# Column 1 of the adjacency matrix in two graph layers: taken ahead of time for rows 8 to 15, in each row's own turn for rows 2 to 7

## The chip, the cores and the metric

The kernel runs on one core of a Trainium2 chip. The metric is the time of one execution on the device in microseconds (us); lower is better. The engines are called by the profile's names: PE (TensorE), its weight loads PEld, DVE (VectorE), ACT (ScalarE), POOL (GpSimd) and SP (SyncE, which issues the transfers here).

## What is computed

```python
def reference(x, adj, u, weight, bias):          # x, u: 8192 x 64, adj: 8192 x 8192, fp32
    keep = (u >= 0.1).astype(x.dtype)
    x_drop = x * keep / (1.0 - 0.1)
    h = layernorm(x + jnp.matmul(adj, x_drop))   # over the 64 features, eps 1e-5
    support = jnp.matmul(h, weight)              # weight: 64 x 64
    return layernorm(h + jnp.matmul(adj, support) + bias)
```

The same matrix `adj` (256 MB) is multiplied with two operands of 64 columns, and the second needs the result of the first. The kernel multiplies `adj` with h first and with the weight at the end.

## The kernel before

**Tiles.** `adj` is cut into 16 x 16 tiles (i, j) of 512 x 512 numbers, 1 MB each. SBUF holds 17 of them (`SLOTS`). For a tile the two layers need x_drop of block j (`stat[..., 0:D]`) and h of block j (`stat[..., D:2 * D]`). h of block i exists only after all 16 tiles of row i have been multiplied with x_drop and the row has had its "turn": PE transposes the sum (line 1017), and DVE and ACT add x and normalise (function `turn`, ending in line 751).

**Jobs.** `order_of_work` writes out one list of jobs that all engines follow:

- `first i j`: layer 1's product of a tile (line 949). `second i j` and `pair i j`: layer 2's product of one tile, or of the tiles (i,j) and (i+1,j) (lines 1002, 996), into one of three banks `echo`, from which DVE joins it to `layer2` (line 656).
- `raw i j` and `fused i j`: both products of a tile with j < i from one load. They are made of seven half products instead of eight by the scheme of Strassen and Winograd: `raw` multiplies the tile as it came (lines 931 to 940), DVE makes sums of the tile's quarters (line 680 ahead of it, lines 692 to 697 after it), and `fused` multiplies those (lines 958 to 966). I call the two together a set. A set also needs sums of the operands x and h of block j, which DVE makes once for a block in three steps (`sum_stat`, lines 668 to 672), behind the turn. After a row's last set DVE combines the products (`combine`).
- `early i j`: both products of the tiles (i,j) and (i+1,j), without sums, before row i's own turn to be worked on (line 982), joined to `layer1` and `layer2`. For column 0 most of this is done in still smaller pieces (`chunk`, `rest`).
- `turn i`, `row_end i`, `combine i`, `final i`.

An fp32 matmul instruction stands in the trace as two records, so a `first` is 8 records, a `pair` 16, an `early` 32.

**What sets the order.** Row by row, `order_of_work` puts six halves of filler around the turn of row i-1 (`FILL`), then the seconds with h of block i-1, then mixes what is left: `heavy` (the sets of row i), `light` (its firsts), `again` (seconds of tiles loaded anew) and `early`. Which comes next depends on `lead`, a running account of work against loads (a tile of load counts 16, an `early` 44, a `fused` 19, a `first` 11): when it is low, heavy and early jobs come first. `with_raw` then moves each raw part ahead of the tile job before its fused part. `place_tiles` gives each tile a slot and makes the list of 346 loads that SP issues in the order of first use (line 495); each waits until the job that used the slot before is done.

**Column 1.** `EARLY = 2`: for rows from 2 on, columns 0 and 1 are not part of the row's own work (`begins_at`). Column 1 is taken by seven `early` jobs, `early 2 1`, `early 4 1`, ... `early 14 1`, which go into the list `early` when h of row 1 is due. So a row's sets begin with column 2, and `has_fused(i)` is true from row 3. The operand sums of even blocks have six places in `stat_homes`, those of odd ones lie in parts of `layer1` whose rows are done with.

Of the kernel before, what the change touches and what calls it, by code (L numbers as in the profile page):

```python
# [35 lines left out]
NB = N // B  # L36
# [4 lines left out]

SLOTS = 17
EARLY = 2
HOMES = (NB - 2 - EARLY) // 2
AHEAD = 3
HOLD = 3
FILL = 6
# [62 lines left out]

def begins_at(i):

    return EARLY if i >= EARLY else 0


def has_fused(i):
    return i > EARLY


def double(i, j):  # L120
# [18 lines left out]
def order_of_work():  # L139

    jobs, again, early = [], [], []
    lead = 0

    def put(job):
        nonlocal lead
        if job[0] == "rest":
            n = 0
        elif job[0] in ("first", "both", "fused", "early", "chunk"):  # L150
            n = len(tiles_of(job))
        else:
            n = sum(not held(*tile) for tile in tiles_of(job))
        lead = max(0, min(LEAD_MOST, lead + WORK[job[0]] - n * WORK_OF_LOAD))
        jobs.append(job)

    groups = NB // PARTS
    chunks_due = []
    for q in range(PARTS):
        for g in range(groups):  # L160
            if g == 0 and q in TURN_FIRST:
                jobs.append(("part_turn", q - 1))
            jobs.append(("part", q, g))
            if g == 0 and q and q not in TURN_FIRST:
                jobs.append(("part_turn", q - 1))
            elif g and chunks_due and (q > 1 or g > 1):
                jobs += chunks_due[:2]
                chunks_due = chunks_due[2:]
            if g == 0 and q:
                chunks_due += chunk_jobs(q - 1)  # L170
        jobs.append(("part_end", q))

    pieces = [[job] for job in chunks_due[:len(chunks_due) % 2]]
    pieces += [chunks_due[n:n + 2] for n in range(len(pieces), len(chunks_due), 2)]
    for i in range(1, NB):
        light = [("first", i, j) for j in range(i + 1, NB) if not held(i, j)]
        near = [("first", i, j) for j in range(NB - 1, i - 1, -1) if held(i, j)]
        if i == 1:
            light.insert(0, ("first", 1, 0))
        heavy = [double(i, j) for j in range(begins_at(i), i - 1) if i >= 2]  # L180
        filler, taken, turned = [], 0, False
        while sum(HALVES[job[0]] for job in filler) < FILL:
            choice = [early] if lead < LEAD and early else [again] if i > 7 else []
            choice = [jobs_of for jobs_of in (*choice, light, again, early, heavy, near) if jobs_of]
            if pieces and (i > 1 or len(filler) % 2 == 0):
                filler += pieces.pop(0)
            else:
                filler.append(choice[0].pop(0))
            for job in filler[taken:]:
                put(job)  # L190
            taken = len(filler)
            if not turned:
                turned = True
                jobs.append(("turn", i - 1) if i > 1 else ("part_turn", PARTS - 1))
        if i == 1:
            late = chunk_jobs(PARTS - 1)
            pieces += [[("early", r, 0)] for r in range(rows_of_chunk((NB - EARLY) // PARTS - 1).stop, NB, 2)]
            pieces += [late[n:n + 2] for n in range(0, len(late), 2)]
            used = len(pieces) - KEPT_PIECES
            for n in range(used):  # L200
                for job in pieces.pop(0):
                    put(job)
                for _ in range(len(light) // (used - n)):
                    put(light.pop(0))
        for job in seconds_of([r for r in range(NB) if held(r, i - 1)], i - 1):
            put(job)
        again += seconds_of([r for r in range(i - 1) if not held(r, i - 1)], i - 1)
        if 1 <= i - 1 < EARLY:
            early = sorted(early + [("early", r, i - 1) for r in range(EARLY, NB, 2)], key=lambda job: job[1:])
        if i >= 2 and begins_at(i) < i:  # L210
            heavy.append(double(i, i - 1))
        summed = not has_fused(i)
        kept = LAST_KEPT if i == NB - 1 else AGAIN_KEPT
        in_a_row = 0
        while True:
            due = [job for job in early if job[1] == i]
            if not (heavy or light or due):
                break
            spare = len(light) + max(0, len(again) - kept) + len(early)
            if heavy and in_a_row * (spare + 1) < len(heavy) and in_a_row < MOST_IN_A_ROW:  # L220
                chosen = heavy
            elif lead < LEAD and (due or heavy or early):
                chosen = early if due else (early or heavy if in_a_row >= MOST_IN_A_ROW else heavy or early)
                if chosen is heavy and in_a_row >= MOST_IN_A_ROW:
                    chosen = light or (again if len(again) > kept else heavy)
            elif len(again) > kept:
                chosen = again
            elif i == NB - 1:
                chosen = light or heavy or early
            else:  # L230
                chosen = light or (early if due else heavy)
            in_a_row = in_a_row + 1 if chosen is heavy else 0
            put(chosen.pop(0))
            if not summed and not any(job[0] == "fused" for job in heavy):
                jobs.append(("combine", i))
                summed = True
        for job in near:
            put(job)
        jobs.append(("row_end", i))
    jobs += again[:1]  # L240
    jobs.append(("turn", NB - 1))
    jobs += again[1:]
    pending = None
    for i in range(NB - 2, -1, -2):
        jobs.append(("pair", i, NB - 1))
        if pending is not None:
            jobs.append(("final", pending))
        pending = i
    jobs.append(("final", pending))
    return with_raw(jobs)  # L250
# [46 lines left out]
def resnorm_graph_layers(nc: bass.Bass, x, xu, adj_t, adj_parts, adj_0, adj_chunks, weight, bias, out):  # L297
# [43 lines left out]
    with ctx:  # L341
# [33 lines left out]
        def layer1_pair(i):  # L375
            return layer1[:, (i - EARLY) // 2]

        def stat_sums(j):


            home = layer1_pair(j) if j % 2 else stat_homes[:, (j - EARLY) // 2]
            return home.rearrange("p (v k f) -> p v k f", v=4, k=2)

        def of_part(q):
# [192 lines left out]
        def _(dve):  # L577
# [176 lines left out]
            for job in jobs:  # L754
# [41 lines left out]
                elif job[0] == "row_end":  # L796
                    i = job[1]
                    dve.wait_ge(turned_ready, turns(i - 1))
                    dve.wait_ge(tile_jobs_done, done_after[job])
                    if i < EARLY:  # L800
                        dve.tensor_copy(halves[D:P, :], sum_f[i % 2][D:P, :]).then_inc(half_by_dve, 1)
                    else:

                        dve.wait_ge(added, n_second)
                        dve.tensor_tensor(out=halves[of_row(i), :], in0=sum_f[i % 2][of_row(i), :],
                                          in1=layer1_pair(i)[of_row(i), :], op=ALU.add).then_inc(half_by_dve, 1)
                elif job[0] == "turn":
                    turn(turns(job[1]) - 1, job[1], slice(0, C))
                    if EARLY <= job[1] < NB - 2:
                        sum_stat(job[1])  # L810
                elif job[0] == "final":
                    n = n_final
                    dve.wait_ge(hb_ready, n + 1)
                    dve.wait_ge(product_ready, n + 1)
                    dve.tensor_tensor(out=output_rows(n), in0=product[n % 2][:, :, 0:D], in1=h_bias[n % 2],
                                      op=ALU.add).then_inc(product_read, 1)
                    if n < len(finals) - 2:
                        norms += 1
                        variance(output_squares(n), var[:, n % 2], 2 * C, scale[:, 1:2])
                        if n >= 2:  # L820
                            dve.wait_ge(y_ready, n - 1)
                        inverse_root(rstd[:, n % 2], var[:, n % 2], root[:, n % 2], newton[:, 0], norms).then_inc(rstd_ready, 1)
                    n_final += 1
# [15 lines left out]
        def _(pe):  # L839
# [15 lines left out]
            def stat_sums_of(j):  # L855

                nonlocal stat_sums_seen
                if j - EARLY + 1 > stat_sums_seen:
                    pe.wait_ge(stat_sums_ready, j - EARLY + 1)
                    stat_sums_seen = j - EARLY + 1  # L860

            def h_of(turned_rows):

# [203 lines left out]
```

## Time and profile before

| | us |
|---|---|
| median of 3 executions | 902.74 |
| their range | 902.63 to 902.84 |
| the profiled execution | 902.77 |
| its span, first to last instruction | 901.0 |
| PE busy | 873.1 (97%) |
| DVE busy | 529.6 (59%) |
| data moved, mean rate over the span | 359.60 MB, 399 GB/s |

The page cuts the span into 40 equal slices of 22.5 us, so its line of GB/s is a curve of the transfers over time. "Busy" of PE is the time in which at least one matmul is in the array by the profile's model; it doesn't say whether a faster PE would end the kernel sooner. For that the chain of waits is read: it goes back from the last instruction, at each step to what released it. Turns are landmarks in time: the transposes of rows 1, 2 and 3 begin at 135.16, 198.95 and 245.63 us.

### The profile page before, as it was taken

The numbers are of one execution on the slowest core, as the hardware profiler recorded it, in microseconds if no ns is written. First come the engines' busy times: TensorE is split into PE (matmuls) and PEld (weight loads), VectorE is DVE, ScalarE is ACT, GpSimd is POOL, SyncE is SP. The second block draws the span as 40 slices with busy tenths as digits, with TensorE's granted clock in tenths as the row PEclk, the third lists the DMA queues.
The fourth block names the chain that finished last, engine by engine and source line by source line (L and its number), as shares of the span: only waits on it lengthen the run. The fifth ranks groups of instructions, "written<-read, shape, count | busy, mean of one in ns | idle before, by whom it ended". The sixth has DMA issues, their size and how long they took to land.

```text
span 901.0 us, 13601 instructions
## 1 busy us (share of the span) xinstructions
PE 873.1 (97%) x5754; PEld 406.1 (45%) x5754; DVE 529.6 (59%) x1026; ACT 30.2 (3%) x74; POOL 25.3 (3%) x24
## 2 busy tenths in 40 slices
PE   3899999999999999999999999999999999999996
PEld 3653333333343444535354554636446456456343
DVE  6356123126145656766676667768677768768655
ACT  0100000000000000000000000000000000000011
POOL 3000000000000000000000000000000000000133
PEclk9999999999999999999999999999999999999998
DMA  9999999999999999999999999989899999999952
GB/s 373 411 416 421 420 420 420 421 421 420 420 420 422 419 420 420 420 401 410 420 420 403 413 404 380 422 352 422 359 408 419 414 417 419 420 421 419 420 242 71
DMA packets 55404, 359.60 MB, mean 399 GB/s; under 512 B 6448, under 2 KB 10544, under 8 KB 12592
## 3 DMA queue, kind: packets, MB, share of 16 engines
q1 hardware_dynamic: 55344, 358.74, 96.7%
q8 instruction: 46, 0.75, 0.3%
q14 instruction: 14, 0.11, 0.0%
HBM read 356.61 MB, written 2.10 MB: 398 GB/s over the span
## 4 chain that ended last, share of the span: by engine, by line
PE 92%; DMA 4%; SPq 2%; issue 1%; DVE 1%; POOLq 0%; POOL 0%; ACT 0%; DVEq 0%
PE psum L996 22%; PE psum L949 21%; PE psum L964 8%; PE psum L931 8%; PE psum L958 8%; PE psum L982 6%; PE psum L917 5%; PE psum L938 4%; PE psum L1002 4%; DMA tiles<-adj_chunks 2%; DMA tiles<-adj_t 2%; PE psum L894 1%; SPq L495 1%; PE psum L1017 1%; PE psum L1032 1%
## 5 line engine op out<-in xcount | busy, mean ns | idle before, releaser
L949 PE MATMUL psum<-tiles,stat 128*64 128x512 f32 x976 | 216.8, 593 | 0.1
L996 PE MATMUL psum<-tiles,stat 128*64 128x512 f32 x944 | 211.7, 594 | 0.0
L656 DVE TENSOR_TENSOR layer<-psum,layer 128x512 f32<-128x512 f32 (+1 forms) x143 | 98.6, 689 | 182.8 <-PE psum L996 85.6
L949 PEld LDWEIGHTS psum<-tiles,stat 128*64 128x64 f32 x976 | 69.6, 137 | 128.2 <-issue 122.5
L996 PEld LDWEIGHTS psum<-tiles,stat 128*64 128x64 f32 x944 | 66.5, 137 | 123.7 <-issue 121.4
L692 DVE TENSOR_TENSOR tiles<-tiles 128x512 f32<-128x512 f32 x90 | 62.2, 691 | 53.7 <-PE psum L940 51.7
L966 PE MATMUL psum<-tiles,stat 128*64 128x256 f32 x360 | 92.7, 380 | 0.0
L933 PE MATMUL psum<-tiles,stat 128*64 128x256 f32 x360 | 92.4, 379 | 0.0
L931 PE MATMUL psum<-tiles,stat 128*64 128x256 f32 x360 | 92.4, 379 | 0.0
L931 PEld LDWEIGHTS psum<-tiles,stat 128*64 128x64 f32 x360 | 49.3, 137 | 40.9 <-issue 20.0
L680 DVE TENSOR_TENSOR tiles<-tiles 128x512 f32<-128x512 f32 x90 | 60.6, 683 | 10.0 <-DMA tiles<-adj_t 10.0
L695 DVE TENSOR_TENSOR tiles<-tiles 128x512 f32<-128x512 f32 x90 | 62.3, 692 | 3.1
L697 DVE TENSOR_TENSOR tiles<-tiles 128x512 f32<-128x512 f32 x90 | 61.6, 684 | 0.0
L982 PE MATMUL psum<-tiles,stat 128*64 128x512 f32 x256 | 56.4, 593 | 2.2 <-issue 2.2
L894 PE MATMUL psum<-tiles,stat 128*64 128x128 f32 x512 | 34.4, 294 | 16.7 <-DMA tiles<-adj_parts 15.1
L933 PEld LDWEIGHTS psum<-tiles,stat 128*64 128x64 f32 x360 | 49.4, 137 | 0.0
L960 PE MATMUL psum<-tiles,stat_homes 128*64 128x256 f32 x192 | 49.3, 379 | 0.0
L964 PE MATMUL psum<-tiles,stat_homes 128*64 128x256 f32 x192 | 49.3, 379 | 0.0
L958 PE MATMUL psum<-tiles,stat_homes 128*64 128x256 f32 x192 | 49.3, 379 | 0.0
L966 PEld LDWEIGHTS psum<-tiles,stat 128*64 128x64 f32 x360 | 48.9, 137 | 0.0
L917 PE MATMUL psum<-tiles,stat 128*64 128x512 f32 x96 | 45.1, 600 | 0.5 <-DMA tiles<-adj_chunks 0.5
L918 PE MATMUL psum<-tiles,stat 128*64 128x512 f32 x96 | 45.1, 600 | 0.0
(100 smaller groups left out, 849.5 us busy)
## 6 DMA issues: line engine op xcount, KB each, us to landing
tiles<-adj_t SPq DMA_DIRECT2D x306, 1024.0 KB, 13.4
tiles<-adj SPq DMA_DIRECT2D x12, 1024.0 KB, 19.2
tiles<-adj_chunks SPq DMA_DIRECT2D x12, 1024.0 KB, 20.4
tiles<-xu SPq DMA_DIRECT2D x4, 1024.0 KB, 7.9
tiles<-adj_parts SPq DMA_DIRECT2D x16, 256.0 KB, 17.7
x_res<-x SPq DMA_DIRECT2D x16, 128.0 KB, 13.9
out<-layer SPq DMA_DIRECT2D x8, 256.0 KB, 2.1
w<-weight SPq DMA_DIRECT2D x4, 16.0 KB, 9.6
```

The costliest lines, as they stand in the source:

```text
L656: return dve.tensor_tensor(out=to, in0=addend, in1=to, op=ALU.add)
L692: dve.tensor_tensor(out=tile[:, top, left], in0=tile[:, top, left], in1=tile[:, top, right], op=ALU.add).then_inc(operands_ready, 1)
L695: dve.tensor_tensor(out=tile[:, bottom, left], in0=tile[:, bottom, left], in1=tile[:, top, left], op=ALU.add).then_inc(operands_ready, 1)
L917: pe.matmul(bank[0:D, :], stat[:, c, half], moving[:, n], start=True, stop=True)
L931: pe.matmul(products[0][low, left], stat[:, j * C + k, 0:D], tile[:, k, left], start=new and k == 0, stop=False, skip_group_check=True)
L933: pe.matmul(products[0][high, left], stat[:, j * C + 2 + k, 0:D], tile[:, 2 + k, left], start=new and k == 0, stop=False, skip_group_check ...
L949: last = pe.matmul(sum_f[i % 2][to, :], stat[:, j * C + c, 0:D], tile[:, c], start=begun.get("f") != i and c < 2, stop=ends and c >= 2, sk ...
L958: pe.matmul(products[1][low, left], t[:, 2, k], tile[:, k, left], start=False, stop=False, skip_group_check=True)
L964: pe.matmul(products[0][low, right], t[:, 1, k], tile[:, 2 + k, right], start=False, stop=False, skip_group_check=True)
L966: last = pe.matmul(products[0][high, right], stat[:, j * C + 2 + k, D:2 * D], tile[:, 2 + k, left], start=False, stop=False, skip_group_ch ...
L982: last = pe.matmul(bank[to, :], stat[:, j * C + c, half], tile[:, c], start=c == 0, stop=c == C - 1)
L996: last = pe.matmul(bank[to, :], stat[:, j * C + c, D:2 * D], tile[:, c], start=c == 0, stop=c == C - 1)
```

## The change

For rows 2 to 7 column 1 becomes part of the row's own work, as a set (raw and fused) like the columns behind it. For rows 8 to 15 it stays with the four `early` jobs `early 8 1` to `early 14 1`. The jobs `early 2 1`, `early 4 1` and `early 6 1` go, six sets come: 96 in place of 90 in the list (the last tile of column 14 is no set in either, though it is one in the title's count, 97 for 91). Row 2 gets a combination. Block 1 gets operand sums, and as `layer1` isn't free for it yet, its sums get a seventh place in `stat_homes`. Nothing else is edited, but `order_of_work` makes another list from it.

```diff
 SLOTS = 17
 EARLY = 2
-HOMES = (NB - 2 - EARLY) // 2
+EARLY_COLUMNS = 1
+LATE_ROWS = 8
+HOMES = (NB - 2 - EARLY) // 2 + 1
...
 def begins_at(i):
 
-    return EARLY if i >= EARLY else 0
+    return EARLY if i >= LATE_ROWS else EARLY_COLUMNS if i >= EARLY else 0
 
 
 def has_fused(i):
-    return i > EARLY
+    return i >= EARLY and i > begins_at(i)
...
-        if 1 <= i - 1 < EARLY:
-            early = sorted(early + [("early", r, i - 1) for r in range(EARLY, NB, 2)], key=lambda job: job[1:])
+        if EARLY_COLUMNS <= i - 1 < EARLY:
+            early = [("early", r, i - 1) for r in range(LATE_ROWS, NB, 2)]
...
-            home = layer1_pair(j) if j % 2 else stat_homes[:, (j - EARLY) // 2]
+            home = layer1_pair(j) if j % 2 and j > EARLY else stat_homes[:, j // 2]
...
-                    if EARLY <= job[1] < NB - 2:
+                    if EARLY_COLUMNS <= job[1] < NB - 2:
                         sum_stat(job[1])
...
-                if j - EARLY + 1 > stat_sums_seen:
-                    pe.wait_ge(stat_sums_ready, j - EARLY + 1)
-                    stat_sums_seen = j - EARLY + 1
+                if j - EARLY_COLUMNS + 1 > stat_sums_seen:
+                    pe.wait_ge(stat_sums_ready, j - EARLY_COLUMNS + 1)
+                    stat_sums_seen = j - EARLY_COLUMNS + 1
```

Three places on PE show how the list moves. Line numbers of the kernel after are two higher. A row counts instructions, so `first` is x4, `pair` x8 and `early` x16 here.

The first place is behind turn 1 (row L1017 or L1019), where row 2 begins. Before:

```order
L1017 MATMUL psum<-ident,halves 128x128 x4
L949 MATMUL psum<-tiles,stat 64x512 x16
L996 MATMUL psum<-tiles,stat 64x512 x8
L982 MATMUL psum<-tiles,stat 64x512 x16
L949 MATMUL psum<-tiles,stat 64x512 x4
L982 MATMUL psum<-tiles,stat 64x512 x16
```

After:

```order
L1019 MATMUL psum<-ident,halves 128x128 x4
L951 MATMUL psum<-tiles,stat 64x512 x16
L933 MATMUL psum<-tiles,stat 64x256
...
L942 MATMUL psum<-tiles,stat_homes 64x256
L998 MATMUL psum<-tiles,stat 64x512 x8
L960 MATMUL psum<-tiles,stat_homes 64x256
...
L968 MATMUL psum<-tiles,stat 64x256
L984 MATMUL psum<-tiles,stat 64x512 x16
L951 MATMUL psum<-tiles,stat 64x512 x8
```

`raw 2 1` now stands ahead of `pair 0 1` (L998), with operand sums of block 1 in its last two products, and `fused 2 1` behind it; the `early` job that follows is `early 8 1`.

The second place is turn 2 and the way to row 3's first set. Before:

```order
L982 MATMUL psum<-tiles,stat 64x512 x16
L1017 MATMUL psum<-ident,halves 128x128 x4
L982 MATMUL psum<-tiles,stat 64x512 x16
L996 MATMUL psum<-tiles,stat 64x512 x8
L931 MATMUL psum<-tiles,stat 64x256
```

After:

```order
L984 MATMUL psum<-tiles,stat 64x512 x16
L1019 MATMUL psum<-ident,halves 128x128 x4
L951 MATMUL psum<-tiles,stat 64x512 x8
L998 MATMUL psum<-tiles,stat 64x512 x8
L933 MATMUL psum<-tiles,stat 64x256
```

Between the turn and `pair 0 2`, which needs h of row 2, two firsts (x8) stand in place of an `early` (x16).

The third place is row 5, behind turn 4. The five firsts after the turn (x20) are `first 5 10` to `first 5 14`. Before:

```order
L1017 MATMUL psum<-ident,halves 128x128 x4
L949 MATMUL psum<-tiles,stat 64x512 x20
L1002 MATMUL psum<-tiles,stat 64x512 x4
L996 MATMUL psum<-tiles,stat 64x512 x8
L931 MATMUL psum<-tiles,stat 64x256
...
L1002 MATMUL psum<-tiles,stat 64x512 x4
L958 MATMUL psum<-tiles,stat_homes 64x256
```

After:

```order
L1019 MATMUL psum<-ident,halves 128x128 x4
L951 MATMUL psum<-tiles,stat 64x512 x20
L1004 MATMUL psum<-tiles,stat 64x512 x4
L998 MATMUL psum<-tiles,stat 64x512 x8
L933 MATMUL psum<-tiles,stat 64x256
...
L1004 MATMUL psum<-tiles,stat 64x512 x4
L933 MATMUL psum<-tiles,stat 64x256
```

Behind the same firsts and `pair 2 4` stand `raw 5 1`, `second 4 4`, `raw 5 2`, `fused 5 1` and `fused 5 2`, where there were `raw 5 2`, `second 4 4` and `fused 5 2`; rows 6 and 7 have the same, with a `pair` or another `second` between the raw parts. From `row_end 7` on the two lists are equal. SP's list of loads has, ahead of tile (5,14), the tiles (2,1) to (7,1) before, and (2,1) to (4,1) after; the tiles (8,1) to (15,1) are ahead of it in both.

## Rows read from the trace of the kernel before

**Rows 1.** page of the profile: busy time, granted clock and transfers in 40 slices

```profile
PE 873.1 (97%) x5754; PEld 406.1 (45%) x5754; DVE 529.6 (59%) x1026; ACT 30.2 (3%) x74; POOL 25.3 (3%) x24
...
PEclk9999999999999999999999999999999999999998
DMA  9999999999999999999999999989899999999952
GB/s 373 411 416 421 420 420 420 421 421 420 420 420 422 419 420 420 420 401 410 420 420 403 413 404 380 422 352 422 359 408 419 414 417 419 420 421 419 420 242 71
```

**Rows 2.** busy time by stretch; the first line names the columns

```profile
core 0: us, PE busy (x) PEld busy (x) DVE busy (x) ACT busy (x) POOL busy (x), PEclk, DMA share, GB/s
...
192.00:242.00 50.00, 50.00 (x248) 18.17 (x249) 18.39 (x40) 0.62 (x2) 0.00 (x0) 1.00 1.01 420
242.00:288.00 46.00, 45.90 (x244) 17.38 (x242) 22.20 (x53) 2.42 (x6) 0.00 (x0) 1.00 1.01 420
288.00:323.00 35.00, 35.00 (x208) 14.83 (x206) 21.66 (x45) 1.21 (x3) 0.00 (x0) 1.00 1.01 420
...
450.00:600.00 150.00, 150.00 (x1036) 74.16 (x1034) 105.39 (x197) 3.64 (x9) 0.00 (x0) 1.00 0.98 400
```

**Rows 3.** chain of waits, 255 to 300 us: start us, us, what

```profile
269.62 17.92 DMA tiles<-adj_t
287.54 0.04 issue
287.58 1.94 PE psum L949 x8
```

**Rows 4.** waits of PE's weight loads, 242 to 288 us: total us, times, longest

```profile
PEld psum L949 <- DMA tiles<-adj_t: 1.6, 3, 1.0
```

**Rows 5.** the same waits, 288 to 870 us

```profile
PEld psum L949 <- DMA tiles<-adj_t: 0.3, 1, 0.3
```

**Rows 6.** waits of SP, 288 to 870 us

```profile
SPq L495 <- PE psum L996: 198.8, 46, 10.0
```

**Rows 7.** page, transfers by what they move: KB each, us to landing

```profile
tiles<-adj_t SPq DMA_DIRECT2D x306, 1024.0 KB, 13.4
```

**Rows 8.** chain of waits: pair 0 1, and an early job

```profile
142.78 3.43 PE psum L996 x16
...
154.80 6.87 PE psum L982 x32
```

**Rows 9.** timeline of PE: raw part, second 2 2, second part, next

```profile
209.82 0.38 PE L931 MATMUL psum<-tiles,stat 128*64 128x256 f32 x1
...
211.12 1.89 PE L1002 MATMUL psum<-tiles,stat 128*64 128x512 f32 x8
212.83 0.38 PE L958 MATMUL psum<-tiles,stat_homes 128*64 128x256 f32 x1
...
214.56 2.31 PE L949 MATMUL psum<-tiles,stat 128*64 128x512 f32 x10
```

**Rows 10.** line 495's transfers, issued 196 to 290 us, then 590 to 600

```profile
DMA to landing us min/median/max: 8.1/13.9/18.7
...
DMA to landing us min/median/max: 4.8/6.8/8.9
```

**Rows 11.** chain of waits, 185 to 200 us: before early 10 1; turn 2

```profile
190.85 1.02 issue
...
198.95 0.59 PE psum L1017 x4
```

**Rows 12.** timeline of DVE in turn 2: joins, h, last operand sum

```profile
198.99 1.42 DVE L656 TENSOR_TENSOR layer<-psum,layer 128x512 f32<-128x512 f32 x2 [7.35 <-PE psum L982]
...
204.29 0.48 DVE L751 SCALAR_TENSOR_TENSOR stat<-work,h_scale,rstd 128x256 f32<-128x256 f32 x1
...
205.59 0.29 DVE L672 TENSOR_TENSOR stat_homes<-stat_homes,stat 128x128 f32<-128x128 f32 x1
```

**Rows 13.** groups by line on DVE, 288 to 360 us: first of three sums

```profile
L692 DVE TENSOR_TENSOR tiles<-tiles 128x512 f32<-128x512 f32 x7 | 4.8, 693 | 3.5 <-PE psum L940 3.3
```

## The prediction

> **What bounds the kernel now.** I read the page's totals first [rows 1]. PE is busy 97% of the span and the granted clock is the upper of its two levels (2.4 GHz) until the last slice, so the first thought is that PE bounds everything and that PE work saved is time saved. The rows on the transfers speak against that for the first third of the span: the 16 DMA engines move 416 to 422 GB/s in every slice from the third to the seventeenth. The stretches [rows 2] show both at once: from 192 to 323 us PE is busy for practically the whole time and the transfers run at 420 GB/s with a share of 1.01. Two resources at their limit need a third view to say which one sets the time. In the chain of waits [rows 3] a single transfer of an adjacency tile takes the chain from 269.62 to 287.54 us, and behind it come eight records of line 949. This is `first 5 14`, the first product of tile (5,14): the chain runs through DMA up to there. The waits say the same: PE's weight loads waited for a tile three times, 1.6 us, between 242 and 288 us [rows 4], and once, 0.3 us, in all of 288 to 870 us [rows 5]. From then on the wait is the other way about: SP waits for PE to free slots, 198.8 us in line 996 alone [rows 6], and the rate falls to 400 GB/s between 450 and 600 us [rows 2].
>
> So there are two regimes, with the border at (5,14). **Before 287.5 us the time is the number of tiles that have to be loaded ahead of (5,14). After it the time is PE's work.** PE work that goes before the border is worth nothing beyond what the queue allows, PE work that comes after it costs its full length.
>
> **The change, part by part.** The prices first. One tile is 1024 KB [rows 7], so 1,048,576 bytes at 420 GB/s [rows 2], 2.50 us. One `early` job (two tiles, both halves) is 32 records of line 982, 6.87 us [rows 8]. One fused set is its raw part, 209.82 to 211.12 us, 1.30 us, and its second part, 212.83 to 214.56 us, 1.73 us [rows 9]: 3.03 us. For two tiles that is 6.06 against 6.87 us.
>
> *Removed on PE:* `early 2 1`, `early 4 1`, `early 6 1`, 3 x 6.87 = 20.6 us. *Added on PE:* sets for (2,1) to (7,1), 6 x 3.03 = 18.2 us. By PE's work alone the change saves 2.4 us (six times one eighth of 3.43 us, the time of a set of full products [rows 8], makes 2.6).
>
> *Moved.* All three removed jobs stood before the border. Of the six sets only (2,1), (3,1) and (4,1) do; (5,1), (6,1) and (7,1) come after `first 5 14`. The same holds for their loads: six tiles were ahead of (5,14) in SP's list, three are now. The number of loads in all stays 346.
>
> *Before the border.* PE would be 20.6 - 9.1 = 11.5 us earlier at (5,14). Its tile is three loads earlier: 3 x 2.50 = 7.5 us. The tile is the later one, so `first 5 14` moves from 287.58 to 280.1 us, and of PE's 11.5 us 4.0 turn into waiting. That holds only if the queue stays full: the time from issue to landing is 8.1 us at the least and 13.9 in the median here, and 4.8 where the queue is empty [rows 10], so an issue may slip by 3 us and more before a landing does.
>
> Where these 4.0 us are spent doesn't matter, but three places can be named. (1) Raw (2,1) now stands ahead of `pair 0 1`, which began at 142.78 us [rows 8]. It needs its tile, two loads nearer to the front than PE is: I put 0.7 us of wait there. It also needs the operand sums of column 1, three new DVE steps. In row 2's turn these end 205.59 + 0.29 - 198.95 = 6.9 us after the transposes begin [rows 11, 12]. The four `first` jobs behind turn 1 cover 6.9 us as well, so this wait lies between 0 and about 0.5 us, below the tile's. (2) `early 12 1` no longer stands between turn 2 and `pair 0 2`; two `first` jobs do, 3.4 us. h of row 2 was ready 204.29 + 0.48 - 198.95 = 5.8 us after the transposes began [rows 11, 12], and the transposes with their lead-in take 0.6 to 0.7. So PE waits 5.8 - 0.7 - 3.4 = 1.7 to 2 us for h, a wait that the kernel before doesn't have. (3) The rest is waits for tiles, as the 1.02 us ahead of `early 10 1` now [rows 11], and most of it just before `first 4 13` and `early 14 1`. By the counts PE still reaches (5,14) about 0.3 us ahead of its tile (bounds -1 to +2); a shortfall is paid at the end one for one.
>
> *After the border.* Three more sets, 3 x 3.03 = 9.1 us, on PE with nothing beside them to wait for: this is on the path. Behind row 7 the order of work is the same as before. Is the queue good for it? Rows 6 and 7 each ask for one tile more, 2.5 us, and PE spends 3.03 us on each: the tiles gain on PE. Nothing.
>
> *DVE.* Each set has four sums of 0.69 us [rows 13], 2.8 us; a combination for row 2 is new (its ops are those of the other rows, some 5 us), and six joins of 0.7 us go. In rows 2 to 4 DVE is busy 18.4 of 50 us [rows 2], and PE has a 6.87 us job behind the new combination: cover enough, and if it were gone it would fall into the 4.0 us. In rows 5 to 7 DVE is at 21.7 of 35 us [rows 2], so 2.8 us a row fit. Between a set's raw part and the middle of its second part PE has 1.7 + 1.3 + 0.9 = 3.9 us in row 5 (a `second`, the next raw part, half of the second part); DVE needs three sums and one join of 1.4 us, 3.5 us. I take 0, with 0 to 2 us for the three rows together. A gain is excluded, since DVE holds nobody up there now. ACT, POOL and SP have no new instructions in their turn.
>
> **The sum.** -7.5 us before the border, +9.1 us after it: +1.6 us. The profiled execution took 902.77 us (span 901.0 and 1.8 around it), which gives 904.4; its distance to the median of 902.74 us is 0.03 us, so I forecast **904.3 us**, with 903.6 to 905.2 for this case alone.
>
> One figure of a load is worth weighing. The rows show 420 GB/s. The Trainium skill ("DMA: Bandwidth & Descriptors", section Bandwidth) gives some 358 GB/s to each core when both of a pair stream and about 425 to one alone. By the lower rate a tile would be 2.9 us, three of them 8.8, and the sum +0.3 us; this trace sides with the higher one.
>
> **The rivals.**
>
> *PE sets the time throughout, faster.* If the tile of (5,14) was late only by chance, the PE work saved counts in full: 902.8 - 2.4 = 900.3 us. For it: PE's 97%. Against it: the landing ends the chain, and the queue has no gap before it. 0.07.
>
> *PE has room behind the border too.* PE's weight loads are busy 45% [rows 1]. If the matmuls could be packed closer, the three late sets would be hidden and the three loads would be the whole difference: 902.8 - 7.5 = 895.3 us. The sets of [rows 9] follow each other without a gap, which speaks against it. The Trainium skill ("Perfetto Trace Analysis", section Identifying the Most-Contended Engine) calls the busy share of matmuls a bad measure and wants the one of LDWEIGHTS; by that reading this rival would be the likely one. 0.02.
>
> *DVE's sums hold up the new sets, slower.* In rows 5 to 7 the sets (i,1) and (i,2) now stand one behind the other, and DVE must have both sets of sums ready. It decides from the point where a join or a turn delays the sums by more than 0.4 us (3.9 against 3.5 above). One late set costs from 0.4 to 2.1 us (three sums); with 0.5 us in each row the time is 904.3 + 1.5 = 905.8 us. 0.17; the wait for h at `pair 0 2` slipping past its cover has the same price and is in this.
>
> *No difference.* The border moves a little instead of holding: with the queue 1 to 2 us faster up to (5,14) than three loads make it, for instance by shorter landings, the sum comes to zero, 902.8 us. 0.08. That the change doesn't do what it says is excluded by the order of its instructions, but for 0.01.
>
> **How the numbers follow.** A measurement of this kernel tells about 0.2% from no change, 1.8 us, so the border to "slower" is at 904.55 us, close above the forecast. The forecast's own case has 0.65; two thirds of it, 0.44, lie below that border and 0.21 above. Same: 0.44 + 0.08 + 0.01 = 0.53. Slower: 0.21 + 0.17 = 0.38. Faster: 0.07 + 0.02 = 0.09. The range goes from 902.0 to 906.2 us: it holds the forecast's case, the case of no difference and the slower rival up to 0.6 us a row, and leaves out the two faster rivals.
>
> **What would show it.** In the profile after, the chain should go through a transfer that ends near 280 us, in front of the `first 5 14`; one wait of about 1.9 us should stand ahead of `pair 0 2`, near 200 us; the turn of row 2 should come some 2.5 us earlier than now, that of row 4 some 7 us, and from row 7 on each turn 1.6 us later, with a constant distance. Lines 931 and 958 (933 and 960 in the new file) should have six sets more. If turn 7 comes earlier than before, the border isn't where I put it; if the distance grows over rows 5, 6 and 7 by more than 3.03 us each, it is DVE; if the chain no longer passes through a transfer near 280 us, PE was late at the border.

## The result and the profile after

| | before | after |
|---|---|---|
| median | 902.84 us (10 executions, 902.63 to 902.94) | 904.96 us (10 executions, 904.83 to 905.14) |
| profiled execution, its span | 902.77, 901.0 | 905.14, 903.0 |

The change makes the kernel 2.1 us slower, a ratio of 1.0024 with a 95% interval of 1.0015 to 1.0032. The forecast was 1.6 us slower. The slowest execution before (902.94) and the fastest after (904.83) lie 1.9 us apart. One of the five executions of the kernel with LATE_ROWS = 16 below was in another state and took 3269.7 us; the other four lie between 908.83 and 909.01.

The page after, against [rows 1]: PE is busy 1.9 us less although the span is 2.0 us longer, and DVE 17.7 us more. The curve of the transfers stays at 415 to 422 GB/s from the third slice to the seventeenth.

```profile
PE 871.2 (96%) x5826; PEld 412.9 (46%) x5826; DVE 547.3 (61%) x1060; ACT 30.2 (3%) x74; POOL 25.3 (3%) x24
...
GB/s 373 412 415 422 421 419 421 421 421 420 420 421 419 421 418 422 419 372 410 420 420 404 408 416 369 420 352 422 368 411 420 411 406 420 418 421 422 419 246 70
```

The chain of waits after, 255 to 300 us (start, duration, what), answers to [rows 3]: the transfer ends at 280.14 and `first 5 14` begins at 280.19 us, 7.4 us earlier than before.

```profile
262.18 17.96 DMA tiles<-adj_t
280.14 0.04 issue
280.19 1.94 PE psum L951 x8
```

The same view between 135 and 150 us shows the wait for tile (2,1) ahead of `raw 2 1`, which the kernel before doesn't have:

```profile
118.39 24.92 DMA tiles<-adj_t
143.31 0.04 issue
143.35 0.43 PE psum L933
...
144.87 3.43 PE psum L998 x16
```

And between 185 and 245 us: a wait before `early 14 1` (it stands where [rows 11] has `early 10 1`), the way of h of row 2 through DVE and ACT to `pair 0 2`, and the transfer of tile (4,13). For the first the profile names no releaser ("issue"); it stands before the `early` job near 190 us in each kernel with full loads that has such a job there, and in none of the three below in which loads are halved, so it is a wait for tiles.

```profile
187.79 1.56 issue
189.35 7.10 PE psum L984 x32
...
201.78 0.50 DVE stat L753
202.27 0.25 issue
202.52 3.65 PE psum L998 x16
...
224.26 18.25 DMA tiles<-adj_t
242.52 0.04 issue
242.56 1.94 PE psum L951 x8
```

A table of landmarks, from the chains and the timelines (us; the last column is the beginning of the last turn's transposes):

| | first 5 14 | turn 7 | turn 15 |
|---|---|---|---|
| before | 287.58 | 394.14 | 843.39 |
| after | 280.19 | 395.89 | 845.37 |
| distance | -7.39 | +1.75 | +1.98 |

From the border to turn 7 the distance grows by 9.14 us, three sets of 3.03 us and 0.05. After that the two kernels do the same work, and it grows by 0.23 more, all of it at one place in row 10 (last section).

### The profile page after: what moved, and what is told of

Its sections match the earlier page's. It is cut to its first block, busy times and chain, and to the rows that moved or that the text cites. A ratio compares the mean times of both kernels' runs of the same rounds, so it can differ in the third digit from the quotient of the medians.

```text
span 903.0 us, 13788 instructions
## 1 busy us (share of the span) xinstructions
PE 871.2 (96%) x5826; PEld 412.9 (46%) x5826; DVE 547.3 (61%) x1060; ACT 30.2 (3%) x74; POOL 25.3 (3%) x24
## 4 chain that ended last, share of the span: by engine, by line
PE 86%; DMA 9%; SPq 2%; issue 1%; DVE 1%; POOLq 0%; ACT 0%; POOL 0%; DVEq 0%
PE psum L998 22%; PE psum L951 17%; PE psum L933 9%; PE psum L966 9%; PE psum L960 9%; DMA tiles<-adj_t 7%; PE psum L940 4%; PE psum L919 4%; PE psum L984 4%; PE psum L1004 4%; DMA tiles<-adj_chunks 2%; PE psum L896 1%; SPq L497 1%; PE psum L1034 1%; PE psum L1019 1%
## 5 line engine op out<-in xcount | busy, mean ns | idle before, releaser
L951 PE MATMUL psum<-tiles,stat 128*64 128x512 f32 x976 | 217.3, 593 | 0.6 <-DMA tiles<-adj_t 0.4
L998 PE MATMUL psum<-tiles,stat 128*64 128x512 f32 x944 | 211.7, 594 | 1.9 <-DVE stat L753 1.9
L658 DVE TENSOR_TENSOR layer<-psum,layer 128x512 f32<-128x512 f32 (+1 forms) x137 | 94.4, 689 | 163.6 <-PE psum L998 82.5
L951 PEld LDWEIGHTS psum<-tiles,stat 128*64 128x64 f32 x976 | 70.8, 137 | 126.3 <-issue 119.1
L998 PEld LDWEIGHTS psum<-tiles,stat 128*64 128x64 f32 x944 | 66.6, 137 | 125.3 <-issue 122.9
L694 DVE TENSOR_TENSOR tiles<-tiles 128x512 f32<-128x512 f32 x96 | 66.3, 691 | 59.4 <-PE psum L942 57.6
L933 PE MATMUL psum<-tiles,stat 128*64 128x256 f32 x384 | 98.6, 379 | 0.5 <-DMA tiles<-adj_t 0.5
L968 PE MATMUL psum<-tiles,stat 128*64 128x256 f32 x384 | 99.0, 381 | 0.0
L935 PE MATMUL psum<-tiles,stat 128*64 128x256 f32 x384 | 98.7, 380 | 0.0
L933 PEld LDWEIGHTS psum<-tiles,stat 128*64 128x64 f32 x384 | 52.5, 137 | 44.1 <-issue 20.5
L682 DVE TENSOR_TENSOR tiles<-tiles 128x512 f32<-128x512 f32 x96 | 64.6, 683 | 11.8 <-DMA tiles<-adj_t 11.8
L697 DVE TENSOR_TENSOR tiles<-tiles 128x512 f32<-128x512 f32 x96 | 66.4, 692 | 3.3
L699 DVE TENSOR_TENSOR tiles<-tiles 128x512 f32<-128x512 f32 x96 | 65.7, 684 | 0.0
L966 PE MATMUL psum<-tiles,stat_homes 128*64 128x256 f32 x216 | 55.5, 379 | 0.0
L962 PE MATMUL psum<-tiles,stat_homes 128*64 128x256 f32 x216 | 55.5, 380 | 0.0
L960 PE MATMUL psum<-tiles,stat_homes 128*64 128x256 f32 x216 | 55.4, 379 | 0.0
L935 PEld LDWEIGHTS psum<-tiles,stat 128*64 128x64 f32 x384 | 52.6, 137 | 0.0
L968 PEld LDWEIGHTS psum<-tiles,stat 128*64 128x64 f32 x384 | 52.0, 137 | 0.0
L919 PE MATMUL psum<-tiles,stat 128*64 128x512 f32 x96 | 45.1, 600 | 0.5 <-DMA tiles<-adj_chunks 0.5
L920 PE MATMUL psum<-tiles,stat 128*64 128x512 f32 x96 | 45.1, 600 | 0.0
L966 PE MATMUL psum<-tiles,layer 128*64 128x256 f32 x168 | 43.4, 381 | 0.0
```

The source lines that it names most:

```text
L658: return dve.tensor_tensor(out=to, in0=addend, in1=to, op=ALU.add)
L694: dve.tensor_tensor(out=tile[:, top, left], in0=tile[:, top, left], in1=tile[:, top, right], op=ALU.add).then_inc(operands_ready, 1)
L697: dve.tensor_tensor(out=tile[:, bottom, left], in0=tile[:, bottom, left], in1=tile[:, top, left], op=ALU.add).then_inc(operands_ready, 1)
L699: dve.tensor_tensor(out=tile[:, bottom, right], in0=tile[:, top, left], in1=tile[:, bottom, right], op=ALU.subtract).then_inc(operands_rea ...
L919: pe.matmul(bank[0:D, :], stat[:, c, half], moving[:, n], start=True, stop=True)
L933: pe.matmul(products[0][low, left], stat[:, j * C + k, 0:D], tile[:, k, left], start=new and k == 0, stop=False, skip_group_check=True)
```

## Experiments

The theory: the time is that of the loads ahead of (5,14) plus that of PE's work behind it. The rivals: PE's work sets the time from end to end; the new wait for h at `pair 0 2` is what costs; DVE's additional sums are what costs. Each group of four (the last of two) ran on one chip, beside the kernel before: 902.80 us for the first, 902.88 for the second, 902.69 for the third.

### How many rows take column 1 in their own turn

Three kernels differ from the kernel after in one number:

```diff
-LATE_ROWS = 8
+LATE_ROWS = 4        # e1_late4;  6 in e2_late6, 16 in e3_late16
```

> Only rows 2 and 3 take column 1 in their own turn (LATE_ROWS = 4); rows 4 to 15 keep it ahead of time. Theory (loads up to (5,14), PE work behind it): both new sets stand ahead of first 5 14 and so do their tiles, so the border has the same 119 loads in front and the same work behind. first 5 14 begins at 287.6 us as in the kernel before, and the time is its 902.8 us within 0.3. Rival (PE's work sets the time throughout): one early job of 6.87 us less, two sets of 3.03 us more, 0.8 us faster, 902.0.

> Rows 2 to 5 take column 1 in their own turn (LATE_ROWS = 6). Theory: of the tiles ahead of (5,14) one, (5,1), moves behind it, so the border comes 2.5 us earlier, at 285.1, and 3.03 us of PE work are added behind it: 0.5 us slower than before, 903.4. Rival (PE throughout): four sets for two early jobs, 1.6 us faster, 901.2.

> All rows from 2 on take column 1 in their own turn, none ahead of time (LATE_ROWS = 16): the same step as the change, taken further. Theory: (5,1) to (15,1), eleven tiles, move behind first 5 14, which then begins 11 x 2.50 = 27.5 us earlier, near 260 us; behind it 11 sets are added, 33.3 us: 5.8 us slower than before, 908.6 (1 us either way, as other waits may come behind the border with so much PE work gone from the rows ahead of it). Rival (PE throughout): 14 sets for seven early jobs, 42.4 for 48.1 us, 5.7 us faster, 897.1. Rival (the change costs by its wait for h at pair 0 2 alone): 902.8 + 1.9 or so, as after the change, since that wait doesn't grow.

| kernel | sets after `first 5 14` | first 5 14 begins | expected | measured | ratio, 95% interval |
|---|---|---|---|---|---|
| LATE_ROWS = 4 | 0 | 287.71 | 902.8 | 903.11 | 1.0004, 0.9995 to 1.0013 |
| LATE_ROWS = 6 | 1 | 285.10 | 903.4 | 903.64 | 1.0009, 1.0000 to 1.0018 |
| after (8) | 3 | 280.19 | 904.3 | 904.96 | 1.0024, 1.0015 to 1.0032 |
| LATE_ROWS = 16 | 11 | 260.16 | 908.6 | 908.90 | 1.0067, 1.0053 to 1.0081 |

Each of these kernels has less work on PE than the one above it in the table, and each takes longer. The rival "PE throughout" gives 902.0, 901.2, 900.3 and 897.1 us; the first lies just outside the interval, the others are refuted clearly, the last by almost 12 us.

The wait for h is refuted as the cause too: with LATE_ROWS = 6 and 16 PE has no wait for DVE between 135 and 400 us, and these kernels are 0.8 and 6.1 us slower than the one before. With 6 the chain goes through the transfer of tile (5,14) as in the kernel after (chain, 260 to 290 us):

```profile
267.04 18.01 DMA tiles<-adj_t
285.06 0.04 issue
285.10 1.94 PE psum L951 x8
```

The row of 4 is weaker evidence than its number suggests. It is 0.31 us over the kernel before, at the edge of what was expected, and no transfer stands at the border in its chain. PE comes to `first 5 14` by its own work and doesn't wait there, and its last waits for tiles are far ahead of it: before `raw 2 1` and, at 187.6 to 189.3 us, before an `early` job. There PE loses 1.4 us more than in the kernel before, where 0.8 us of its work were saved. So this kernel shows that the PE work saved isn't won, but it doesn't show that the tile (5,14) holds the time. The view of PE's waits from 135 to 400 us (total us, times, longest) has only these:

```profile
PE psum L984 <- issue: 1.6, 1, 1.6
PE psum L933 <- DMA tiles<-adj_t: 0.6, 1, 0.6
```

In the kernel with 16 PE's weight loads wait 22 times for a tile before the border. This adds nothing to the price by the count of loads: it is the waiting for the same loads, in small pieces. The waits of PE's weight loads from 85 to 262 us (total us, times, longest) are these:

```profile
PEld psum L951 <- DMA tiles<-adj_t: 25.0, 22, 1.8
```

The chain goes through the tile (5,14) there too, at the time that the count of loads gives (27.5 us earlier than 287.6):

```profile
242.12 18.00 DMA tiles<-adj_t
260.12 0.04 issue
260.16 1.94 PE psum L951 x8
```

### The wait for h at pair 0 2

The kernel after, with the long job behind the turn instead of ahead of it:

```diff
+    jobs.remove(("early", 14, 1))
+    jobs.insert(jobs.index(("turn", 2)) + 1, ("early", 14, 1))
+    jobs.remove(("first", 3, 7))
+    jobs.insert(jobs.index(("turn", 2)), ("first", 3, 7))
     return with_raw(jobs)
```

> The kernel after, with early 14 1 put behind turn 2 and first 3 7 ahead of it, so that 6.87 + 1.72 us of work cover the 5.8 us until h of row 2 is there. Theory: the wait of 2 us at pair 0 2 goes, and comes back as waits for tiles before first 4 13; first 5 14 still begins near 280.2 us, and the time stays at 905.0 within 0.3. Rival (the wait for h is what costs): 2 us faster, 903.0.

Measured: 905.07 us, ratio 1.0025 (1.0016 to 1.0035), the time of the kernel after. `pair 0 2` began at 201.20 instead of 202.52 us and no longer waited for h, but `first 4 13` began at 242.58 and `first 5 14` at 280.19 us, as in the kernel after. The 2 us came back as waits for tiles: 0.8 us more before `early 14 1`, the rest before the firsts that end with `first 4 13`. The row of PE's weight loads over the whole span has 8 waits of 6.8 us in place of 5 and 3.8:

```profile
PEld psum L955 <- DMA tiles<-adj_t: 6.8, 8, 1.4
```

So with full loads this wait costs nothing.

### Without the loads in the way

Here the tiles of rows 2 to 4 that a `first` uses are loaded by half, in three kernels: the one before, the one after and the one of e4_swap. The instructions on PE and DVE stay, but with half of each of these tiles left out the results aren't those of the reference.

```diff
+                if kind == "first" and 2 <= tile[0] <= 4:
+                    to, source = to[:, 0:2], source[:, 0:2]
                 sp.dma_start(to, source).then_inc(s_part[part] if part else s_arrived[slot], 16)
```

> The kernel before, in which the tiles of rows 2 to 4 that a first uses are loaded by half (0.5 MB; the other half keeps what the slot held, so the products of these tiles are not the reference's). PE's and DVE's work is the same. That takes some 39 x 1.25 us of transfers from the stretch up to 287 us. Theory: the border is gone and PE sets the time from row 2 on; what is gained is only what PE waited for tiles there, 1.2 us before early 10 1 and 0.3 before first 5 14: 901.3 us. It is the base for the next two.

> The kernel after with the same tiles loaded by half (their products are again not the reference's). Theory: PE's waits for tiles from row 2 on (0.7, 1.7, 0.6 and 0.3 us) go, the 2.1 us at pair 0 2 for h stay and now count in full: 905.0 - 3.3 = 901.7 us, 0.2 to 0.5 us over the lightened kernel before (which is -2.5 of PE work, +2.1 for h and some 0.3 of bubbles). Rival (the three sets behind the border cost for another reason than the loads, for instance DVE's sums): the distance to the lightened kernel before stays at 2.1 us, 903.4.

> The kernel of e4_swap (early 14 1 behind turn 2) with the same tiles loaded by half (not the reference's products there). Theory: with neither the loads nor the wait for h in the way, the PE work that the change saves comes out: 901.7 - 2.0 = 899.7 us, some 1.8 to 2.4 us under the lightened kernel before. Rival (the change saves nothing on PE): no less than the lightened kernel before, 901.3.

| kernel, lightened | expected | measured | turn 7 in the profile |
|---|---|---|---|
| before | 901.3 | 901.07 | 392.66 |
| after | 901.7 | 901.37 | 392.16 |
| after with e4's swap | 899.7 | 899.33 | 390.12 |

Against the full kernel before the ratios are 0.9981 (0.9972 to 0.9990), 0.9984 (0.9975 to 0.9993) and 0.9962 (0.9949 to 0.9974). In the lightened kernel before the transfers have room, above all in the second stretch; the columns are those of [rows 2]:

```profile
85.00:192.00 107.00, 105.58 (x490) 35.63 (x491) 24.54 (x50) 2.26 (x6) 0.00 (x0) 1.00 0.97 391
192.00:288.00 96.00, 96.00 (x494) 35.45 (x492) 41.12 (x94) 3.05 (x8) 0.00 (x0) 1.00 0.74 270
```

The distance of the change, 2.1 us with full loads, is 0.3 us without them, and with the wait for h gone too it is -1.7 us by the medians. By turn 7 of the profiles it is -2.54 us, and the count of PE's work is -2.4. Between -1.7 and -2.54 stand the 0.2 us of row 10 (last section) and the profiled execution of the lightened kernel before, which at 901.40 us lay 0.3 over its median; the rest, some 0.25 us, is open. DVE does all its new sums in these kernels, so they are not what costs. So the change does save the PE work that it says, it opens a wait of 2 us for h, and in the full kernel both disappear in front of the border. In the lightened kernel after, the wait for h stands as before, now with its full price. The chain, 195 to 204 us:

```profile
199.04 0.50 DVE stat L755
199.54 0.25 issue
199.78 3.65 PE psum L1000 x16
```

### Moving the border

PE has work around the border that needs no load: the seconds of row 5's turn, on tiles that are kept. If it stands ahead of the last tiles instead of behind them, the queue should bind less. In the kernel after:

```diff
+    for late in (("first", 5, 13), ("first", 5, 14)):
+        jobs.remove(late)
+    jobs[jobs.index(("pair", 2, 4)) + 1:jobs.index(("pair", 2, 4)) + 1] = [("first", 5, 13), ("first", 5, 14)]
     return with_raw(jobs)
```

> The kernel after with first 5 13 and first 5 14 put behind pair 2 4, with full loads. 5.2 us of PE work that need no load (second 1 4 and pair 2 4, on tiles kept in SBUF) now stand ahead of the tile that ends the queue. Theory: the wait before first 5 14 (0.3 us) goes and the border moves on to the firsts of row 6, which have 1.1 us of slack now; PE reaches its turns 0.3 to 0.6 us earlier than in the kernel after: 904.4 to 904.7 us. Rival (the loads don't bind at (5,14)): no change, 905.0, or slower if h of row 4 is not ready for second 1 4 any more.

Measured: 904.56 us, ratio 1.0019 (1.0011 to 1.0028), 0.4 us under the kernel after. Turn 7 began at 395.56 instead of 395.89 us, which is the wait of 0.3 us before `first 5 14`: in this trace PE waits for no tile between `first 4 13` (242.6 us) and 400 us. By the medians 0.4 us is little more than the 0.2 us that separate the kernel before on one chip from itself on another, so it is support and no proof.

The same in the kernel before, first at row 5 alone, then at rows 5 and 6:

```diff
+    for late, behind in (
+            (('first', 5, 14), ('pair', 2, 4)),
+            (('first', 5, 13), ('pair', 2, 4)),
+            (('first', 6, 15), ('pair', 2, 5)),      # not in e9_move_row5
+            (('first', 6, 14), ('pair', 2, 5)),      # not in e9_move_row5
+    ):
+        jobs.remove(late)
+        jobs.insert(jobs.index(behind) + 1, late)
     return with_raw(jobs)
```

> The kernel before, with first 5 13 and first 5 14 put behind pair 2 4 and nothing else. Theory: the wait before first 5 14 (0.3 us) goes, but the firsts of row 6 have only 0.5 us of slack in the kernel before, so the queue binds there next, at first 6 15: 902.8 us, at most 0.2 faster. Rival (the wait at (5,14) alone sets the time): 0.3 to 0.5 faster, 902.4.

> The kernel before, with first 5 13 and first 5 14 behind pair 2 4, and first 6 14 and first 6 15 behind pair 2 5: at both places where the queue binds, PE work that needs no load stands ahead of the last tiles. Theory: the queue sets the time only up to row 2, and what PE waited for tiles behind it and what the loads held it back come out: 0.7 to 1.0 us faster than before, 901.9 us. Rival (order within a row doesn't matter, since the number of loads is the same): 902.8.

Measured: 902.53 and 902.54 us, both 0.9998 (0.9989 to 1.0007): no difference from the kernel before, and none between the two. For e9 that was expected, for e10 it was 0.6 us too hopeful. The expectation is at fault, not the count: PE waits only 0.3 us before `first 5 14` in the kernel before. The one wait of [rows 5] behind it is of a weight load alone, and PE's matmuls go on without a gap there. So 0.3 us was all there was to gain, and I had priced it by what I thought the loads held back beyond that. In both kernels PE has no wait for a tile from 193 to 400 us: in the kernel before the loads and PE's work reach (5,14) within 0.3 us of each other, and moving that border alone wins next to nothing. In e10's chain no transfer stands at the border any more; the last wait for a tile is that before `early 10 1`, 0.3 us longer than in [rows 11] in this execution, which takes back what was won (185 to 200 us):

```profile
190.74 1.31 issue
192.05 7.09 PE psum L990 x32
```

No kernel here is clearly faster than the one before.

## Why the prediction was right

**The border.** Right, to the transfer. The step that named (5,14) as the tile in front of which the time is counted in loads and behind which it is counted in PE's work holds in the profiles of the kernels before, with LATE_ROWS = 6, after and with LATE_ROWS = 16. They have 119, 118, 116 and 108 loads ahead of it, and `first 5 14` begins behind the landing of its tile at 287.6, 285.1, 280.2 and 260.2 us, 2.5 us for each load. With LATE_ROWS = 4 the beginning, 287.7 us, fits the count, but PE doesn't wait for the tile there. In the kernel before the border decides over 0.3 us only, since PE comes to it almost as late as the tile; it is by the change, which frees PE of more work than it takes loads away, that it becomes the limit for all that was saved.

**PE's work ahead of it.** 11.5 us less, of which 7.5 come through and 4.0 turn into waiting. Measured: 7.4 come through. The waits in that stretch, each with the few hundredths that PE loses in starting again, are 0.8 before `raw 2 1`, 1.8 before `early 14 1`, 2.1 at `pair 0 2`, 0.6 and 0.3 before `first 4 13` and `first 5 14`, 5.6 us in all, against 1.2 before `early 10 1` and 0.3 before `first 5 14` in the kernel before: 4.1 us more, and 11.5 - 4.1 = 7.4.

**The three places.** (1) 0.7 us at `raw 2 1`, for its tile, as forecast; the operand sums were there in time. (2) 1.7 to 2 us at `pair 0 2`: it began 6.15 us after the transposes of turn 2 (196.37 to 202.52 us), against 4.1 us of cover, 2.0 to 2.1 us. (3) PE's lead at the border was forecast as 0.3 us, and the wait before `first 5 14` is 0.3 us.

**Behind the border.** 9.1 us forecast, 9.14 measured. e5 to e7 show that a set costs what its rows say, and that it is 0.4 us cheaper than its share of an `early` job.

**DVE.** No price forecast, with 0 to 2 us for rows 5 to 7. Measured there: 0.05 us. The sums of (5,2) come less than 0.1 us late, and the slower rival, which needed more than 0.4 us of delay, didn't come true. The lead was as thin as the text says: the next set in the row waits for its sums seven times over the whole kernel now and five times before, 2.4 us of weight loads in place of 1.6.

**What the sum missed.** 0.5 us between 1.6 and 2.1, so the size came out less well than the mechanism. 0.1 is the border's 7.4 for 7.5, 0.05 is DVE, and 0.23 arises in row 10, where nothing is changed. The rest, some 0.1 us, is the distance between profiled executions and medians. The step that was mis-sized is "Behind row 7 the order of work is the same as before", taken to mean that the time is too.

**The rivals.** "PE sets the time throughout" had 0.07 and is refuted by e2, the kernel after and e3. The rival in which PE has room behind the border (0.02) is refuted by the same rows: eleven sets behind the border are paid in full, while the weight loads are busy 46% of the span. In this kernel the busy share of the weight loads is no sign of room on PE. The Trainium skill ("Perfetto Trace Analysis", section Identifying the Most-Contended Engine) names that share, beside the share of the peak arithmetic, as the measure to go by; the trace doesn't agree for the share, with 46% and no room.

By the prediction's own line, 904.55 us, the measured 904.96 us is "slower", to which it gave 0.38, against 0.53 for "same". The forecast lay 0.25 us under the line and the result 0.4 us over it, and the interval of the ratio holds both sides of 0.2%. So on which side of the line the forecast fell was decided by the 0.5 us that the sum missed, and not by the mechanism.

## What to carry to other kernels

When two resources are both busy all the time, look in the chain of waits for the last transfer, and count differently on its two sides (and after a change look again whether it is still there, as with LATE_ROWS = 4 it wasn't): loads in front of it, work behind it. A saving of work in front of that border is worth nothing beyond what the loads allow, and a step that takes a load out of the front and puts its work behind the border costs the difference of the two (here 3.03 - 2.50 us a tile), even if it is less work in all. A wait that a change opens in front of the border costs nothing as long as the queue stays full (the 2 us for h here), so don't mend it first.

## What the hardware showed that was not expected

In row 10 the first sum behind a raw part starts 0.4 us later than the rows account for. In the kernel before, DVE sat idle for 1.00 us ahead of it, after the change 1.37 us, though PE's raw part ends in the same way (timelines of DVE, before and after):

```profile
527.04 0.69 DVE L692 TENSOR_TENSOR tiles<-tiles 128x512 f32<-128x512 f32 x1 [1.00 <-PE psum L940]
```

```profile
529.16 0.69 DVE L694 TENSOR_TENSOR tiles<-tiles 128x512 f32<-128x512 f32 x1 [1.37 <-PE psum L942]
```

The row's last set then waits 0.2 us for its sums. It isn't a chance event of one execution: from turn 7 to turn 10 the five kernels with LATE_ROWS = 8 take 146.64 to 146.66 us (the kernel after, e4, e6, e7, e8), with or without full loads, and those with the order before or LATE_ROWS = 4 and 6 (before, e1, e2, e5, e9, e10) take 146.43 to 146.44. What the five share is the number of DVE instructions ahead of this place: in the trace of the kernel after, with those counted that only wait for a semaphore (the counter by which one engine waits for another), 703 stand ahead of the late sum, and 664 ahead of the same sum in the kernel before. PE isn't the cause. The instruction just ahead of the sum is one that waits for PE's semaphore, and the sum starts 0.46 us behind the start of that instruction, where in the kernel before it is 0.10 us.

The same delay moves about in other kernels. In the kernel before it is at 625.77 us, 0.45 us behind such an instruction, and PE loses nothing by it. With LATE_ROWS = 4 it is at another sum, at 612.05 us, ahead of which DVE is idle for 1.05 us instead of the 0.70 us of the kernel before. There row 12 takes 0.20 us longer, two thirds of the 0.31 us by which that kernel is slower.

```profile
625.77 0.69 DVE L692 TENSOR_TENSOR tiles<-tiles 128x512 f32<-128x512 f32 x1 [0.41 <-DVE tiles L680]
```

```profile
612.05 0.69 DVE L694 TENSOR_TENSOR tiles<-tiles 128x512 f32<-128x512 f32 x1 [1.05 <-PE psum L942]
```

Ahead of each of these two sums stand exactly 831 DVE instructions, though they are different sums. In the kernel after a second one, at 760.28 us, is late by 0.35 us against the kernel before, with 1087 ahead of it; 703, 831 and 1087 lie 128 and 256 apart. So this delay goes with the place in DVE's stream of instructions and not with the job. Whether the fetching of instructions is behind it isn't shown by any row, and it was not tried; the packets of the queues that the page calls "instruction" start at 524.3 and 532.5 us around the place at 529.16, and none at it.
